# Both choices of a token sent back to back by half groups, first loads of a stage issued by the stage before, and a final sum by half groups, in a layer of two mixtures of experts around linear attention

## The reference

```python
x = x + 0.5 * ffn(LN(x))
x = x + attention(LN(x))
x = x + 0.5 * ffn(LN(x))
```

## Time and profile before

| | |
|---|---|
| time, median of 3 runs | 983.95 us (983.07 to 985.2) |
| the profiled execution | 988.44 us, of which the span of the profile is 986.7 us |
| PE busy | 792.0 us, 80% of the span (weight loads 705.0 us) |
| DVE, ACT, POOL busy | 579.8, 470.2, 562.8 us (59%, 48%, 57%) |
| DMA | 90.45 MB, 92 GB/s over the span |
| TensorE's granted clock | 0.914 on average |

### The profile page before, as it was taken

One profiled execution on the slowest core, in us unless ns is written; L12 is line 12 of the kernel. 1 busy time (PEld: TensorE's weight loads), 2 busy tenths in 40 slices (PEclk: granted clock), 3 DMA queues, 4 the chain that ended last, 5 costly groups with the idle time before them and its releaser, 6 DMA issues. The chain is left out here.

```text
span 986.7 us, 20333 instructions
## 1 busy us (share of the span) xinstructions
PE 792.0 (80%) x5348; PEld 705.0 (71%) x5349; DVE 579.8 (59%) x2112; ACT 470.2 (48%) x967; POOL 562.8 (57%) x584
## 2 busy tenths in 40 slices
PE   2899899847999999806788999899934999999920
PEld 2677777737999999804567777787824999999910
DVE  7688876624555555545557776666722555555536
ACT  3356556313555555415456657665302555555500
POOL 1347777762777777722044266575772777776730
PEclk9799999977999999958779999999976999999965
DMA  9912221132333333241021111010132333333349
GB/s 274 141 45 72 65 68 54 52 92 72 100 105 100 105 101 96 83 164 63 1 65 60 49 44 39 31 48 31 50 97 60 96 101 100 103 102 99 96 166 374
DMA packets 83816, 90.45 MB, mean 92 GB/s; under 512 B 20391, under 2 KB 69421, under 8 KB 82733
## 3 DMA queue, kind: packets, MB, share of 16 engines
q1 hardware_dynamic: 64046, 45.41, 18.3%
q0 software_dynamic: 17408, 35.95, 10.8%
q10 hardware_dynamic: 2304, 8.39, 2.1%
HBM read 47.45 MB, written 44.37 MB: 93 GB/s over the span
## 5 line engine op out<-in xcount | busy, mean ns | idle before, releaser
L1246 POOL DMA_INDIRECT ys<-e_y,e_x x288 | 276.5, 960 | 132.0 <-issue 89.0
L346 POOL DMA_INDIRECT xs<-f_xrow,f_slot x256 | 254.0, 992 | 131.9 <-issue 72.8
L1365 PE MATMUL e_py<-w,e_at 97*128 (+1 forms) x1152 | 152.1, 274 | 0.0
L1365 PEld LDWEIGHTS e_py<-w,e_at 97*128 97x128 f32 (+1 forms) x1152 | 139.9, 191 | 0.1
L1270 DVE TENSOR_TENSOR e_a<-e_pu,e_sil 128x352 f32<-128x352 f32 x144 | 75.6, 525 | 98.2 <-ACT e_sil L1296 96.9
L1277 DVE TENSOR_SCALAR e_y<-e_py,e_x 128x128 f32<-128x128 f32 x288 | 87.8, 347 | 58.9 <-PE e_py L1365 57.9
L1290 ACT ACTIVATE e_xth<-e_px 128x256 fp32r<-128x256 f32 x144 | 55.4, 385 | 131.3 <-PE e_px L1329 130.6
L1296 ACT ACTIVATE e_sil<-e_pu 128x352 f32<-128x352 f32 x144 | 66.9, 464 | 91.0 <-PE e_pu L1342 91.0
L1028 PEld LDWEIGHTS f_pz<-sw,f_gated 128*128 128x128 f32 (+1 forms) x768 | 99.4, 191 | 11.4 <-issue 3.2
L1340 PE MATMUL e_pu<-w13h,e_xth 128*128 x288 | 107.2, 372 | 0.0
L843 ACT ACTIVATE f_sil<-f_phg,sb 128x512 f32<-128x512 f32 (+1 forms) x96 | 65.0, 684 | 84.4 <-PE f_phg L1014 83.7
(11 more groups left out here) (166 smaller groups left out, 1362.7 us busy)
## 6 DMA issues: line engine op xcount, KB each, us to landing
e_x<-xs SPq DMA_DIRECT2D x288, 65.0 KB
f_yt<-ys SPq DMA_DIRECT2D x16, 512.0 KB, 4.6
c_yt<-ys SPq DMA_DIRECT2D x8, 1024.0 KB, 10.4
ys<-e_y,e_x POOLq DMA_INDIRECT x288
xa<-in_attn_x ACTq DMA_DIRECT2D x8, 512.0 KB, 10.2
xs<-f_xrow,f_slot POOLq DMA_INDIRECT x256, 2.3
out<-xa ACTq DMA_DIRECT2D x8, 512.0 KB
f_raw<-in_ffn_w SPq DMA_DIRECT2D x32, 88.0 KB
```

The source lines that it names most:

```text
L346: pool.indirect_dma_start(xs, bass.IndirectOffsetOnAxis(slot[:, q, i:i + 1], 0), xrow[:, i, :], None).then_inc(done, 16)
L1246: pool.indirect_dma_start(ys, bass.IndirectOffsetOnAxis(xin[r][:, t, D:D + 1].bitcast(I32), 0), y[r][:, t, :], None).then_inc(sent[r], 16)
L1365: last = pe.matmul(p_y[r][:, t * D:(t + 1) * D], at[r][0:rows_, q], w2, start=c == 0, stop=c == 1, skip_group_check=True)
```

## The change

Second choices are sent directly behind first ones, by chunks: `send` takes a chunk of 4 tiles, `second_choice(g)` follows `first(g)` in POOL's order, and `rewrite` takes a chunk, waits for that chunk's four sends, and is called in DVE's step for the group before (front 0: between the gates; front 1: the first half near the end of the group's own step, the second half behind `phi_q` of the next). In front 1 `shifts(f)` also moves ahead of `residual(b)`, `shifts_a` behind two of `phi_k`, and POOL's `scales` ahead of `first`. SP loads the first four pairs of an expert stage at the end of the front, behind the pads and behind a wait for all second sends, and the first four chunks of `ys` for front 1 and for `combine` at the end of the expert stage, behind the last scatters. The buffers of these loads (`k.xin`, `k.yt`) live through the whole kernel; in front 0 the raw weights lie in `k.yt`, in front 1 `xt_a` lies in `k.xin`. `combine` works by chunks: 16 loads of 0.5 MB in 12 buffers, twice 16 adds, 16 stores.

```diff
+AHEAD = 4
...
+        k.xin = sb("xin", [P, AHEAD, 2, ROW])
+        k.yt = sb("yt", [P, 4, CHUNK, 2 * D])
+        k.x_in = [[sem(f"x{n}_in{r}") for r in range(RING)] for n in range(2)]
+        k.y_in = [[sem(f"y{n}_in{r}") for r in range(4)] for n in range(2)]
...
+def load_x(nc, sp, k, n, xin, xs, first, pairs, free=None, turn=None):
+
+    _, at = nc.values_load_multi_w_load_instructions(
+        k.tile_at[0:1, ds(first, 2 * len(pairs))], engines=[mybir.EngineType.SP],
...
+    for q, r in enumerate(pairs):
+        if free is not None:
+            sp.wait_ge(free[r], turn)
+        for t in range(2):
+            sp.dma_start(xin[r][:, t], slot_rows(xs)[:, ds(at[2 * q + t], 1)].rearrange(
+                "p j c -> p (j c)")).then_inc(k.x_in[n][r], 16)
+
+
+def load_y(sp, ys, c, buffer, done):
+
+    sp.dma_start(buffer, ys[:, c // 2, c % 2 * CHUNK:(c % 2 + 1) * CHUNK]).then_inc(done, 16)
...
-        sent0 = [sem(f"f{n}_sent0{r}") for r in range(3)]
+        sent0 = [sem(f"f{n}_sent0{r}") for r in range(4)]
...
-                    for c in range(CHUNKS):
-                        wait(sp, x2r, c - 3)
-                        sp.dma_start(yt[c % 4][:], ys[:, c // 2, c % 2 * CHUNK:(c % 2 + 1) * CHUNK]
-                                     ).then_inc(y_in[c % 4], 16)
+                    for c in range(4, CHUNKS):
+                        sp.wait_ge(x2r, c - 3)
+                        load_y(sp, ys, c, yt[:, c % 4], y_in[c % 4])
...
                 sp.wait_ge(pads, 16 * E)
+                sp.wait_ge(sent1, 16 * TILES)
+                load_x(nc, sp, k, n, [k.xin[:, r] for r in range(AHEAD)], xs, 0, range(AHEAD))
...
-                def send(g, q, done):
-                    for i in range(g * GT, (g + 1) * GT):
+                def send(c, q, done):
+                    for i in range(c * CHUNK, (c + 1) * CHUNK):
...
-                    send(g, 0, sent0[g % 3])
+                    for c in (2 * g, 2 * g + 1):
+                        send(c, 0, sent0[c % 4])
...
-                    pool.wait_ge(rewrote, g + 1)
-                    pool.sem_inc(passed, 1)
-                    send(g, 1, sent1)
+                    for c in (2 * g, 2 * g + 1):
+                        pool.wait_ge(rewrote, c + 1)
+                        pool.sem_inc(passed, 1)
+                        send(c, 1, sent1)
...
                 if n == 0:
-                    for g in range(GROUPS + 1):
+                    for g in range(GROUPS):
                         first(g)
-                        second_choice(g - 1)
+                        second_choice(g)
                 else:
-                    for s in range(-3, GROUPS + 2):
-                        first(s - 1)
+                    for s in range(-3, GROUPS):
                         if 0 <= s + 1 < GROUPS:
                             scales(s + 1)
+                        first(s)
                         if s + 3 < GROUPS:
                             scales_a(s + 3)
-                        second_choice(s - 2)
+                        second_choice(s)
...
-                def rewrite(g):
-                    dve.wait_ge(sent0[g % 3], 16 * GT * (g // 3 + 1))
-                    dve.wait_ge(exp2, g + 1)
+                def rewrite(c):
+                    if not 0 <= c < CHUNKS:
+                        return
+                    part = slice(c * CHUNK, (c + 1) * CHUNK)
+                    dve.wait_ge(sent0[c % 4], 16 * CHUNK * (c // 4 + 1))
+                    dve.wait_ge(exp2, c // 2 + 1)
...
+                    rewrite(2 * (s - 1))
                     gates(m + 1)
                     outs(2 * (s - 1) - 1)
                     if s == GROUPS:
                         tables_out()
                     gates(m + 2)
-                    if s >= 2:
-                        rewrite(s - 2)
+                    rewrite(2 * (s - 1) + 1)
...
                 def step_1(s):
...
-                    if 0 <= s + 2 < GROUPS:
-                        shifts_a(s + 2)
                     if attending:
                         phi_q(a, 0)
                         phi_q(a, 1)
+                    rewrite(2 * (s - 1) + 1)
+                    if attending:
                         phi_k(a, 0)
                         phi_k(a, 1)
+                    if 0 <= s + 2 < GROUPS:
+                        shifts_a(s + 2)
...
                     gates(m + 2)
-                    if 0 <= s - 2 < GROUPS:
-                        rewrite(s - 2)
+                    if attending:
+                        shifts(f)
                     if b < GROUPS:
                         residual(b)
                     gates(m + 3)
-                    if attending:
-                        shifts(f)
                     if s == GROUPS:
                         tables_out()
...
                     gates(m + 5)
+                    rewrite(2 * s)
                     if gating:
                         low(2 * s + 1)
...
-        xin = [sb(f"e{n}_x{r}", [P, 2, ROW], ctx=ctx) for r in range(RING)]
+        xin = [k.xin[:, r] for r in range(AHEAD)]
+        xin += [sb(f"e{n}_x{r}", [P, 2, ROW], ctx=ctx)[:] for r in range(AHEAD, RING)]
+        x_in = k.x_in[n]
...
-                load(0, None)
+                load_x(nc, sp, k, n, xin, xs, 2 * AHEAD, range(AHEAD, RING))
                 with sp.Fori(1, PAIRS // RING) as i:
-                    load(2 * RING * i, 32 * i)
+                    load_x(nc, sp, k, n, xin, xs, 2 * RING * i, range(RING), sent, 32 * i)
+                for r in range(RING):
+                    sp.wait_ge(sent[r], 32 * (PAIRS // RING))
+                for c in range(4):
+                    load_y(sp, ys_v, c, k.yt[:, c], k.y_in[n][c])
...
-        yt = [sb(f"c_yt{r}", [P, GT, 2 * D], ctx=ctx) for r in range(4)]
-        in_ready = [sem(f"c_in{r}") for r in range(GROUPS)]
+        yt = [k.yt[:, c] for c in range(4)]
+        yt += [sb(f"c_yt{r}", [P, CHUNK, 2 * D], ctx=ctx)[:] for r in range(8)]
+        in_ready = k.y_in[1] + [sem(f"c_in{c}") for c in range(4, CHUNKS)]
...
-                for g in range(GROUPS):
-                    if g >= 4:
-                        sp.wait_ge(ysum, g - 3)
-                    sp.dma_start(yt[g % 4][:], ys[:, g]).then_inc(in_ready[g], 16)
-                sp.wait_ge(stored, 16 * GROUPS)
+                for c in range(4, CHUNKS):
+                    wait(sp, ysum, c - 11)
+                    load_y(sp, ys, c, yt[c % 12], in_ready[c])
+                sp.wait_ge(stored, 16 * CHUNKS)
...
```

More of the change, by code:

```diff
@@ L133, in build, with slot_rows @@
         front(nc, k, sb, ps, 0, xa, xs_dram, w)
-        experts(nc, k, sb, ps, 0, xs_dram, ys_dram)
+        experts(nc, k, sb, ps, 0, xs_dram, ys_dram, ys_v)
         front(nc, k, sb, ps, 1, xa, xs_dram, ys=ys_v)
-        experts(nc, k, sb, ps, 1, xs_dram, ys_dram)
-        combine(nc, sb, xa, ys_v, out_v)
+        experts(nc, k, sb, ps, 1, xs_dram, ys_dram, ys_v)
+        combine(nc, k, sb, xa, ys_v, out_v)
+def slot_rows(xs):
+    return xs.rearrange("(j p) c -> p j c", p=P)
+def load_x(nc, sp, k, n, xin, xs, first, pairs, free=None, turn=None):
+    _, at = nc.values_load_multi_w_load_instructions(
+        k.tile_at[0:1, ds(first, 2 * len(pairs))], engines=[mybir.EngineType.SP],
+        min_val=0, max_val=E * RTILES + E - 1,
+        skip_runtime_bounds_check_because="a tile of a region, or of the first "
+        "padding tiles: fewer than 16 tiles are left over")
+    for q, r in enumerate(pairs):
[6 more added lines that the diff above has]
+    sp.dma_start(buffer, ys[:, c // 2, c % 2 * CHUNK:(c % 2 + 1) * CHUNK]).then_inc(done, 16)
 def front(nc, k, sb, ps, n, xa, xs, w=None, ys=None):
@@ L195, in front @@
             p_b = ps("f1_pb", [P, 512], ctx)
-            y_in = [sem(f"f1_y{r}") for r in range(4)]
         names = ("ysum", "x2r", "stats_a", "aggr_a", "var_a", "rstd_a", "nmr_a", "xhr_a", "qmm",
@@ L1202, in experts @@
             sem(f"e{n}_{s}") for s in names)
-        x_in = [sem(f"e{n}_in{r}") for r in range(RING)]
         sent = [sem(f"e{n}_sent{r}") for r in range(RING)]
-        rows = xs.rearrange("(j p) c -> p j c", p=P)
         LOOPED = (PAIRS - RING) // RING
@@ L1221, in _ @@
             def _(sp):
-                def load(first, free):
-                    _, at = nc.values_load_multi_w_load_instructions(
-                        k.tile_at[0:1, ds(first, 2 * RING)], engines=[mybir.EngineType.SP],
-                        min_val=0, max_val=E * RTILES + E - 1,
-                        skip_runtime_bounds_check_because="a tile of a region, or of the first "
-                        "padding tiles: fewer than 16 tiles are left over")
-                    for r in range(RING):
-                        if free is not None:
-                            sp.wait_ge(sent[r], free)
-                        for t in range(2):
-                            sp.dma_start(xin[r][:, t], rows[:, ds(at[2 * r + t], 1)].rearrange(
-                                "p j c -> p (j c)")).then_inc(x_in[r], 16)
```

(14 more changed lines are left out.)

41 lines of the change are left out of this document (22 added, 19 removed).

## The result

The changed kernel takes 989.73 us (median of 8 runs, 986.5 to 992.66), the kernel before 984.88 us (8 runs, 981.48 to 986.06). The ratio is 1.0045, with an interval of 1.0026 to 1.0065. The forecast was 964.7 us, 955 to 975.

What follows compares the result with a forecast made beforehand. A row of stages closed by barriers, one queue late at each seam; -6.9 + 1.0 - 0.9 - 5.1 + 0.4 - 5.9 - 1.9 = -19.3, so 983.95 - 19.3 = 964.7 us, range 955 to 975.

Steps and rivals of the forecast that it cites:

- step 0: Opening step of the second front: DVE's wait for first choices, sent before the attention chain, costs +0.4 us (0 to +2).
- First seam: First front's table to PE's restart: POOL stops being last, PE starts at 220.0, not 226.88; -6.9 us (-7.8 to -6.3).
- Waits in the first front: DVE waits inside its step for each half of first choices to land, seven steps: +1.0 us (0 to +4).
- just fits: Both fronts: sends land about when DVE reaches the second half's rewrite, at 68.2 against 68.59 in the first front.
- Second front, steps 1 to 6: Moved shifts save PE 1.1 us a step, a rewrite in the attention chain costs 0.25: -5.1 us (0 to -6.6).
- Third seam: End of the second front to PE's restart: earlier restart despite DVE's waits in steps 7 and 8; -5.9 us (-3.7 to -11.3).
- Second seam: End of the first expert stage: SP issues y loads before the barrier instead of behind it; -0.9 us (-1.0 to 0).
- Final sum: Last stage: starts 0.9 us earlier, with shorter adds and store behind the last load; -1.9 us (-0.5 to -3).
- eight more loads cost nothing: Final sum: 0.5 MB loads issued together overlap, so halving the loads adds no time; the skill's rule would cost 16 us.
- A: Rival: new waits eat the second front's gain, steps 1 to 6 give 0, third seam -3.7; 972.0 us, chance 0.18.
- C: Slower rival: send landings get long, each microsecond beyond 2.3 costs one in 16 steps; 996.7 us at 4.3, chance 0.05.
- B: Rival: DVE's waits cost nothing because POOL's sends start and land a little earlier; -27.6, 956.4 us, chance 0.12.

Runs made afterwards that it cites:

- the late rewrites: Changed kernel with only DVE's rewrites moved to later places of its steps in both fronts, where sends should have landed: 960.46 us, ratio 0.9742 against the kernel before.

## Why the prediction was wrong

The step that failed is the price of DVE's waits for sends. The forecast counted some 7 us for them in all (1.0 in the first front, 0.4 in step 0, 5.4 in front of the second table). The changed kernel had 27.5 us of them, and it became 29.3 us faster without them. The parts in turn:

**First seam** (-6.9): right, -7.4. Which queue would be last, and its parts, were as forecast. What was not seen is that four pairs are more than PE needs at its start. "They land while the barrier closes" is true, but the barrier closes behind their issues.

**Waits in the first front** (+1.0): this step failed first, at +7.6 in this profile, 9.0 and 11.1 in two others with the same first front. It said that the second half's rewrite "just fits", with the median landing of 2.3 us. The median was right, 2.4 in the changed kernel from 55 to 205, but a wait for four sends ends with the last of them to land, and the longest landing there was 3.9. Where DVE waited, it went on 2.3 to 3.9 us behind the start of the last of the four sends (69.70 less 66.18 is 3.5). The six waits of steps 2 to 8 add up to 4.8 us. The rest of the 7.6 is largely PE's lower clock, for which the sum had no term: step 4, in which DVE waited for no send, grew by 3.1 us at 0.80.

**Second front, steps 1 to 6** (-5.1): the gain was there, but +2.2 was measured. The moved shifts are worth 7.4 us in the old order, more than the 6.6 at the end of the range, but that is luck in part: the forecast took PE's wait of one row, 1.09, for every step, PE's idle time shrank by only 2.9, and 4.5 came from the clock, for which the sum had no term. The sentence about the rewrite in the attention chain, "whose wait just fits", failed: there were waits of over half a microsecond in four of the six stretches between slots, up to 3.27 us and 12.2 in all, and taking them away gave 9.0 us (192.28 to 183.33). The longest of them, with the 1.20 behind it, is that of step 0, for which +0.4 was counted. The median landing is 2.3 here too, but the longest is 7.0, and DVE went on up to 4.8 us behind the last of four sends. Ahead of the first slots the front became 1.7 us shorter, which no term forecast. "POOL's square roots ... leave room" was right only because the change also moves the attention's shift, and the forecast did not say so.

**Third seam** (-5.9): -12.3 from table to PE, but +4.3 in the last step and +8.1 up to the table, together +0.1. The waits of steps 7 and 8 were foreseen: the second one was forecast to end 12.6 us behind the slots and ended at 13.6. What failed is "PE has then run ahead, which gives back about 2.2": PE stood still for 2.45 and 2.88 us instead, and the clock that followed made the rest of the way to the table 12.4 us long where 7.9 were counted.

**Second seam** (-0.9): the direction was right; -1.7 up to the first add is outside the range of -1.0 to 0, and the early loads alone gave -0.9. **Final sum** (-1.9): +0.6. The issue did come 1.0 us earlier behind the last scatter. The step "eight more loads cost nothing" failed: halves moved 354 GB/s and whole groups 404 as long as loads ran nearly alone. The rule of the Trainium skill, page "DMA: Bandwidth & Descriptors", section "Rules for kernel authors", at least 1 MiB in a DMA, pointed the right way. By the runs it is worth about 1.6 us here, a tenth of the 16 that the prediction worked out with the fixed cost.

**The rivals.** A named the place, but stopped at a gain of 12: it let the waits eat gains up to there, while they cost some 29. C came nearest, with landings of 3.5 us as the point from which it decides. Its price of one for each microsecond holds in total, 29.3 us for 27.5, but not by stage: about 1.7 in the first front, where the clock fell, 0.7 in steps 1 to 6 and 1.0 behind them. B, in which the waits cost nothing, is what the late rewrites made true: 956.4 forecast, 960.46 measured.

## What to carry to other kernels

A wait inside the queue of the engine that feeds all others can cost as much as it lasts, or more, and partly in a later step: ask how many products queue behind it, and what PE does meanwhile. Where the time of a stretch changes, split it into PE's work and PE's idle time, since the clock can add to a gain or hide a loss. Where a wait "just fits" by a median, put the waiting instruction a few microseconds later and let the queue with slack, here POOL's, pay. And of loads drawn in front of a barrier, draw at most what is needed at once behind it, since every issue holds the barrier up; here two pairs were no better than none.

## What was not expected of the hardware

A stall of 1.14 us on DVE cost 4.9 us in one execution, 3.65 of them in the step behind it, at a granted clock of 0.80, after PE had idled 2.46 us; a gap of 1.13 at the same place left the clock at 1.00. The steps of the second front repeat closely where nothing waits: 183.33, 183.33, 183.29, 183.29, 183.32 and 183.27 us for its six steps in the six kernels that have the late rewrites and both shifts moved. And with DMA full by its share in both, loads of 0.5 MB moved 354 GB/s where loads of 1 MB moved 404.
